# A gather ring of 16 slots: SyncE marks its slots in groups of four instead of one by one

## The reference

```python
def _rgcn_conv(x, W, Wroot, b, src, dst, etype):
    xs = x[src]                          # one row of 256 for each edge
    seg = dst * R + etype                # R = 8 relations
    sums = jax.ops.segment_sum(xs, seg, num_segments=N * R)
    cnt = jax.ops.segment_sum(jnp.ones_like(xs[:, 0]), seg, num_segments=N * R)
    mean = (sums / jnp.maximum(cnt, 1.0)[:, None]).reshape(N, R, -1)
    return x @ Wroot + b + jnp.einsum('nrd,rde->ne', mean, W)
# x + conv(relu(conv(layernorm(x)))), then a top-2 mixture of experts on top of it
```

## Time and profile before

| | us |
|---|---|
| Median of 3 runs | 2933.71 (2932.59 to 2935.83) |
| Profiled execution, span from the first to the last instruction | 3487.9 |
| PE busy (matmul) | 2472.0 (71%) |
| DVE busy | 1780.8 (51%) |
| ACT busy | 1225.2 (35%) |
| POOL busy | 1862.5 (53%) |
| Gathers of the two layers, busy on POOL | 1526.9 (1584 of them) |

### The profile page before, as it was taken

The page is one execution under the profiler, slowest core; times in us unless marked ns, Lnnn a source line. Parts: engine busy times, 40 slices in busy tenths (PEclk is TensorE's granted clock), DMA queues, the critical chain, the costliest instruction groups (busy, mean ns, idle before and its releaser), DMA issues.

```text
span 3487.9 us, 82172 instructions
## 1 busy us (share of the span) xinstructions
PE 2472.0 (71%) x19212; PEld 1832.7 (53%) x19213; DVE 1780.8 (51%) x4984; ACT 1225.2 (35%) x2344; POOL 1862.5 (53%) x1980
## 2 busy tenths in 40 slices
PE   1346787678687786346776587687877428999999
PEld 0113565356365564114564365465656327888887
DVE  7324455345355454124454354354545338787777
ACT  5202343134243342012343143152432126555554
POOL 1666566655655554666556656655563543333333
PEclk9557999589799898557998798798997559999999
DMA  6223323233332232223333333333335234322222
GB/s 216 80 83 112 88 87 91 85 87 89 87 88 87 86 89 64 86 84 97 98 104 97 94 100 99 94 105 95 101 100 163 102 115 132 96 73 71 71 70 59
DMA packets 165489, 333.24 MB, mean 96 GB/s; under 512 B 36078, under 2 KB 102346, under 8 KB 165288
## 3 DMA queue, kind: packets, MB, share of 16 engines
q0 software_dynamic: 91632, 247.48, 24.1%
q1 hardware_dynamic: 39912, 41.03, 4.0%
q10 hardware_dynamic: 33872, 43.92, 3.9%
HBM read 285.39 MB, written 49.07 MB: 96 GB/s over the span
## 4 chain that ended last, share of the span: by engine, by line
PE 44%; issue 22%; DVE 10%; another core or an unknown queue 9%; DVEq 7%; SPq 2%; ACT 2%; DMA 1%; ACTq 0%; POOLq 0%; POOL 0%
PE more_banks L1408 13%; PE sum_banks L1384 9%; PE sum_banks L1385 7%; PE more_banks L1535 4%; PE sum_banks L1535 3%; PE more_banks L1400 3%; PE sum_banks L1545 3%; DVEq L1044 3%; DVEq L1041 2%; DVE sels L1044 2%; DVEq L1027 1%; DVE stage L1079 1%; DVE sels L1036 1%; PE sum_banks L1426 1%
## 5 line engine op out<-in xcount | busy, mean ns | idle before, releaser
L509 POOL DMA_INDIRECT ring<-table,tabs x1584 | 1526.9, 964 | 1046.4 <-SPq L399 670.0
L1384 PE MATMUL sum_banks<-ring,sels 128*128 x2348 | 726.6, 311 | 630.1 <-issue 420.1
L1408 PE MATMUL more_banks<-weights,stage 128*128 128x256 f16 x5292 | 919.1, 290 | 22.0 <-issue 21.4
L1385 PE MATMUL sum_banks<-ring,sels 128*128 x2348 | 732.2, 313 | 41.5 <-issue 38.7
L1384 PEld LDWEIGHTS sum_banks<-ring,sels 128*128 128x128 f16 (+1 forms) x2348 | 242.4, 103 | 928.2 <-issue 896.9
L683 ACT ACTIVATE stage<-sum_banks,inv 128x256 f16<-128x256 f32 x784 | 328.1, 473 | 789.5 <-issue 384.9
L1408 PEld LDWEIGHTS more_banks<-weights,stage 128*128 128x128 f16 x5292 | 531.1, 104 | 135.3 <-issue 37.1
L1036 DVE SCALAR_TENSOR_TENSOR sels<-lane,win_off,tabs 128x256 f16<-128x256 f16 x792 | 349.4, 482 | 422.1 <-remote 181.9
L654 ACT ACTIVATE stage<-more_banks 128x1024 f16<-128x1024 f16 x392 | 402.0, 1026 | 419.1 <-remote 405.6
L1044 DVE TENSOR_SCALAR sels<-lane,win_off,tabs 128x128 f16 x780 | 260.6, 334 | 495.8 <-issue 339.6
L1079 DVE SCALAR_TENSOR_TENSOR stage<-sum_banks,inv,stage 128x256 f16<-128x256 f32 x784 | 347.0, 479 | 57.2 <-issue 40.2
(11 more groups left out here) (319 smaller groups left out, 2407.5 us busy)
## 6 DMA issues: line engine op xcount, KB each, us to landing
ring<-table,tabs POOLq DMA_INDIRECT x1584
weights<-L_ffn_W ACTq DMA_DIRECT2D x96, 178.5 KB
stage<-L_ffn_W ACTq DMA_DIRECT2D x16, 1024.0 KB, 5.0
edge_work<-lot_in SPq DMA_DIRECT2D x54, 260.0 KB
table<-edge_work ACTq DMA_DIRECT2D x49, 128.0 KB
lot_in<-sels SPq DMA_DIRECT2D x8, 260.0 KB
weights<-L_gnn_W SPq DMA_DIRECT2D x2, 1024.0 KB, 8.3
weights<-L_gnn_W ACTq DMA_DIRECT2D x2, 1024.0 KB
```

The lines of the kernel that those rows point to most:

```text
L509: pool.indirect_dma_start(ring_rows[:, b % RING, 0:2 * D], None, tables[layer], bass.IndirectOffsetOnAxis(row_tab[:, b:b + 1], 0)).then_in ...
L1384: pe.matmul(to[:, 0:D + 1], hot, ring_row[:, ds(at + D, D + 1)], start=first, stop=last, skip_group_check=True)
L1385: return pe.matmul(to[:, 0:D], hot, ring_row[:, ds(at, D)], start=False, stop=last, skip_group_check=True)
L1408: return [pe.matmul(ps_out[par], rows[:, xp * KD + k, :], w16[:, wp, k, r * D:(r + 1) * D], start=part == PART_ORDER[0] and n == 0, stop=p ...
```

## The change

SP marks four slots at once. The 16 slots are four groups of four (`GROUP`, `RING_GROUPS`). The four gathers of a group count on one semaphore, and `landed(g)` waits until it has the 64 counts of all four and adds four to `rows_ready`. `freed(g)` waits for the last step that reads the last block of the group (the table keeps every fourth entry only) and adds four to `slots_free`. The order is `freed(g)`, `landed(g + 2)`: two groups, eight blocks, as before. POOL waits before every fourth gather only, and then until all four slots are free. The number of turns of SP's loop stays 48, with four registers to load in place of 16. PE and DVE have the same instructions and the same waits as before. Later users of the gathers' semaphores (`scattered`) have other start values.

```diff
-    AHEAD = RING // 2
+    GROUP = 4
+    RING_GROUPS = RING // GROUP
+    AHEAD = RING_GROUPS // 2
...
-        gathered = [sem(f"gathered{s}") for s in range(RING)]
+        gathered = [sem(f"gathered{g}") for g in range(RING_GROUPS)]
...
-                def landed(turn, s):
-                    sp.wait_ge(gathered[s], turn * 16 + 16 * (USES[s] * layer + 1))
-                    sp.sem_inc(rows_ready[layer], 1)
+                def landed(turn, g):
+                    sp.wait_ge(gathered[g], turn * (16 * GROUP) + 16 * GROUP * (USES[g] * layer + 1))
+                    sp.sem_inc(rows_ready[layer], GROUP)
 
-                def freed(s):
-                    sp.wait_ge(steps_done[layer], sp.snap(regs[s], donate=True) & MASK)
-                    sp.sem_inc(slots_free[layer], 1)
-                for s in range(AHEAD):
-                    landed(0, s)
+                def freed(g):
+                    sp.wait_ge(steps_done[layer], sp.snap(regs[g], donate=True) & MASK)
+                    sp.sem_inc(slots_free[layer], GROUP)
+                for g in range(AHEAD):
+                    landed(0, g)
...
                 with sp.Fori(0, TURNS) as u:
-                    sp.load(regs, free_meta[0:1, ds(u * RING, RING)])
-                    for s in range(RING):
-                        freed(s)
-                        landed(u if s < AHEAD else u + 1, (s + AHEAD) % RING)
+                    sp.load(regs, free_meta[0:1, ds(u * RING_GROUPS, RING_GROUPS)])
+                    for g in range(RING_GROUPS):
+                        freed(g)
+                        landed(u if g < AHEAD else u + 1, (g + AHEAD) % RING_GROUPS)
...
                 for b in range(GATHERS):
-                    if b >= RING:
-                        pool.wait_ge(slots_free[layer], b - RING + 1)
+                    if b >= RING and b % GROUP == 0:
+                        pool.wait_ge(slots_free[layer], b - RING + GROUP)
                     pool.indirect_dma_start(ring_rows[:, b % RING, 0:2 * D], None, tables[layer],
-                                            bass.IndirectOffsetOnAxis(row_tab[:, b:b + 1], 0)).then_inc(gathered[b % RING], 16)
+                                            bass.IndirectOffsetOnAxis(row_tab[:, b:b + 1], 0)).then_inc(gathered[b % RING // GROUP], 16)
...
-            act.activation(free_meta, free_row[:, 0:GATHERS], ACT.Copy).then_inc(tabs_set, 1)
+            act.activation(free_meta, free_row[:, GROUP - 1:GATHERS:GROUP], ACT.Copy).then_inc(tabs_set, 1)
```

More of the change, by code:

```diff
@@ L45, in build_program @@
     GATHERS = BLOCKS + COUNT - 1
-    TURNS = (GATHERS - RING) // RING
-    OVER = GATHERS - RING - TURNS * RING
-    USES = [len(range(s, GATHERS, RING)) for s in range(RING)]
+    assert GATHERS % GROUP == 0
+    GROUPS_ALL = GATHERS // GROUP
+    TURNS = (GROUPS_ALL - RING_GROUPS) // RING_GROUPS
+    OVER = GROUPS_ALL - RING_GROUPS - TURNS * RING_GROUPS
+    USES = [len(range(g, GROUPS_ALL, RING_GROUPS)) for g in range(RING_GROUPS)]
     LOOKS = WINDOWS + 2 * COUNT
@@ L121, in build_program @@
         key_tab = tabs[:, GATHERS:3 * GATHERS + 4]
-        free_meta = tabs[0:1, 2 * GATHERS + 4:3 * GATHERS + 4].bitcast(i32)
+        free_meta = tabs[0:1, 2 * GATHERS + 4:2 * GATHERS + 4 + GROUPS_ALL].bitcast(i32)
         win_off = sb("win_off", [P, WINDOWS + 4])
@@ L306, in build_program @@
         routed, zs_ready = sem("routed"), sem("zs_ready")
-        assert len(set(USES[0:GROUPS])) == 1
-        spots_after = 16 * USES[0] * 2
+        assert GROUPS <= RING_GROUPS
+        spots_after = [16 * GROUP * n * 2 for n in USES]
         scattered = gathered[0:GROUPS]
@@ L390, in _ @@
             for layer in range(2):
-                regs = [sp.alloc_register(f"sp_free{layer}_{s}") for s in range(RING)]
-                def landed(turn, s):
-                    sp.wait_ge(gathered[s], turn * 16 + 16 * (USES[s] * layer + 1))
-                    sp.sem_inc(rows_ready[layer], 1)
-                def freed(s):
-                    sp.wait_ge(steps_done[layer], sp.snap(regs[s], donate=True) & MASK)
-                    sp.sem_inc(slots_free[layer], 1)
-                for s in range(AHEAD):
-                    landed(0, s)
+                regs = [sp.alloc_register(f"sp_free{layer}_{g}") for g in range(RING_GROUPS)]
+                def landed(turn, g):
[6 more added lines that the diff above has]
+                    landed(0, g)
                 if layer == 0:
@@ L404, in _ @@
                 with sp.Fori(0, TURNS) as u:
-                    sp.load(regs, free_meta[0:1, ds(u * RING, RING)])
-                    for s in range(RING):
-                        freed(s)
-                        landed(u if s < AHEAD else u + 1, (s + AHEAD) % RING)
[L409 to L414, removed]
+                    sp.load(regs, free_meta[0:1, ds(u * RING_GROUPS, RING_GROUPS)])
+                    for g in range(RING_GROUPS):
+                        freed(g)
+                        landed(u if g < AHEAD else u + 1, (g + AHEAD) % RING_GROUPS)
+                sp.load(regs, free_meta[0:1, TURNS * RING_GROUPS:(TURNS + 1) * RING_GROUPS])
+                for n in range(TURNS * RING_GROUPS, GROUPS_ALL - AHEAD):
+                    if n < TURNS * RING_GROUPS + OVER:
+                        freed(n % RING_GROUPS)
+                    landed((n + AHEAD) // RING_GROUPS, (n + AHEAD) % RING_GROUPS)
+                sp.sem_inc(rows_ready[layer], GROUP)
                 for r in regs:
@@ L437, in _ @@
             for g in range(GROUPS):
-                sp.wait_ge(scattered[g], spots_after + 32 * CHUNK * len(range(g, CHUNKS, GROUPS)))
+                sp.wait_ge(scattered[g], spots_after[g] + 32 * CHUNK * len(range(g, CHUNKS, GROUPS)))
             def load_lot(row):
@@ L1151, in z_rows @@
                 if c >= GROUPS:
-                    v.wait_ge(scattered[g], spots_after + 32 * CHUNK * (c // GROUPS))
+                    v.wait_ge(scattered[g], spots_after[g] + 32 * CHUNK * (c // GROUPS))
                 for i in range(CHUNK):
```

## The result

The changed kernel takes 2959.7 us (median of 4 runs, 2956.8 to 2962.1), the kernel before on the same chip 2933.7 us: ratio 1.0087, 95% interval 1.0073 to 1.0101. That is +26 us, where +13 us was forecast.

What follows compares the result with a forecast made beforehand. It took the timed runs as near POOL's floor of 1.25 us a gather, 989 us a layer. The middle of 18 us (lag account) and 7.6 us (ends) gave +13 us, 2947 us; 8-in-10 range 2922 to 2982 us.

Steps and rivals of the forecast that it cites:

- the check: Whole kernel: both layers at 989 us plus the first profile's other stretches give 2944 us, 10 us over the timed median.
- Parts 1, 2 and 5: SP's fewer marks, POOL's fewer waits, and the shared semaphore, register loads and table: no gain or cost.
- Part 3: `landed` waits for four gathers: a group's first block is marked up to 3.8 us later, so PE falls further behind.
- The term of the ends: At each layer's end the late landing lies on the path: 3.8 us, twice 7.6 us.
- account of the lag: PE's lag behind POOL over nine runs of tiles, limited by landing and ring: 9 us a layer, 18 us in all.
- costs nothing: Rival: PE never far enough ahead to miss three blocks, ring never full; 2934 to 2939 us, chance 0.22.
- every handover counts: Rival: each change between dense and thin runs costs 3.8 us; 34 us a layer, 68 us, 3002 us; chance 0.08.
- Taking the middle between 18 and 7.6 us: Total: between the lag account's 18 us and the ends alone, 7.6 us, if the ring is never full: +13 us.
- first case: Small loss at the layers' ends and partly in the ring: 2940 to 2958 us, chance 0.45.
- the shorter landing of 2.3 us: The skill's estimate for 128 KB against the trace's 2.9 us; said to move the sum by less than 1 us.
- DVE holding the transposes: Rival: DVE stands in `more_blocks` and PE's transposes wait, 36 us a layer; up to 2990 us, chance 0.05.
- Faster by relieving SP: Rival: POOL's slot waits are partly SP's lateness, half given back by one mark for four; 2916 us, chance 0.20.

Runs made afterwards that it cites:

- second profile: The kernel before, unchanged, profiled again; it spans 2933.1 us, where its first profile spans 3487.9 us.
- experiment 6: The changed kernel with `landed` marked three groups past the freed one in place of two; +27.0 us over the kernel before.
- the two halves: The kernel before with only `landed` marked by fours, +8.4 us, and with only `freed` marked by fours, +10.8 us.
- experiment 1: The kernel before with only `landed` marked by fours, each slot's own semaphore kept, `freed` slot by slot; +8.4 us, ratio 1.0034.

## Why the prediction came out as it did

**What bounds the kernel: right.** The gathers follow each other at little more than 1.25 us: layer 1 of the changed kernel is 1008.9 us where 791 x 1.25 = 989. The floor itself was set somewhat low. It went by the usual gather of 0.95 us, where the earlier trace rows have 964 ns on the average; with that it is 1000 us a layer, and the check would have come out at 2966 us, 32 us over the median in place of 10, a sign that something else in it was too long. The chain that ended last, by line, kernel before (second profile) and changed kernel:

```profile
by line: POOL ring L509 29.3%; issue 15.7%; PE sum_banks L1545 7.9%; PE more_banks L1408 7.3%; DMA ring<-table,tabs 5.2%; PE sum_banks L1384 4.3%; PE sum_banks L1535 4.0%; PE more_banks L1535 3.9%; POOL lot_in L533 3.3%; PE sum_banks L1385 
```

```profile
by line: POOL ring L513 28.0%; issue 14.9%; PE more_banks L1412 10.7%; PE sum_banks L1549 8.1%; PE sum_banks L1388 5.4%; PE sum_banks L1539 3.9%; PE more_banks L1539 3.9%; PE sum_banks L1389 3.8%; POOL lot_in L537 3.2%; PE more_banks L1404 
```

POOL's gathers lead it in both. What grows is PE's dense product, from 7.3% to 10.7% of the span: the path runs longer over PE before it goes back to POOL, as one would expect of a shallower ring.

**Parts 1, 2 and 5, at nothing: right as far as the runs can tell.** Groups of two cost +3.8 us with half of SP's marks, and gathers without a wait have the same 0.30 us in front as those with one.

**Part 3, landing late by 3.8 us at each handover: right in kind.** It was read directly as 15.5 to 19.2 us of lag.

**The term of the ends, 2 x 3.8 us: wrong.** Where PE waits for rows at the last gather, the layer would end later. It doesn't: with landing by four the gap from the last gather to the next layer is 23.2 us, as before,

```profile
1122.24 0.94 POOL L511 DMA_INDIRECT ring<-table,tabs  x1 [0.30 <-issue]
1145.42 1.14 POOL L511 DMA_INDIRECT ring<-table,tabs  x1 [22.23 <-DMA table<-edge_work]
```

and with freeing by four it is shorter, 20.5 us, since PE is less far behind.

```profile
1125.88 0.94 POOL L510 DMA_INDIRECT ring<-table,tabs  x1 [0.30 <-issue]
1146.40 1.13 POOL L510 DMA_INDIRECT ring<-table,tabs  x1 [19.58 <-DMA table<-edge_work]
```

PE is behind POOL at the ends of the layers, the rows had landed, and the term is 0. The sign that the prediction named for itself, a longer stretch between the layers, did not come. Its account of the lag had this the right way round, with a lag at the end of 17 us in place of 21. The row that said so was in hand: POOL had waited 1.5 us for a slot before the last gather, which the rival "costs nothing" used and the sum did not.

**The account of the lag, 18 us for both layers: right in kind, short in size, and wrong in taking both layers alike.** PE's surplus over POOL in tiles 36 to 42 was put at 20 us in both. ACT's copies of the turned means at the first and last couple of these tiles in the second profile of before, layer 0 and then layer 1:

```profile
804.63 1.03 ACT L654 ACTIVATE stage<-more_banks 128x1024 f16<-128x1024 f16 x1
...
901.25 1.02 ACT L654 ACTIVATE stage<-more_banks 128x1024 f16<-128x1024 f16 x1
...
1842.77 1.03 ACT L654 ACTIVATE stage<-more_banks 128x1024 f16<-128x1024 f16 x1
...
1930.64 1.02 ACT L654 ACTIVATE stage<-more_banks 128x1024 f16<-128x1024 f16 x1
```

From the first to the last of 28 couples it is 96.6 us in layer 0, 3.58 us each, and 87.9 us in layer 1, 3.25 each. At that pace 28 couples take 100 and 91 us, and POOL needs 62 x 1.25 = 78 us. So PE's surplus is 23 us in layer 0 and 14 us in layer 1. The other thin runs, read in the same way, have 24, 25 and 25 us in layer 0 and 14, 13 and 15 us in layer 1. Between least and most lag the prediction had 21 us for the ring before and 13 us after. In layer 0 the surplus is over both, so that what the groups take of the ring is lost at each thin run; in layer 1 it is well below the first and only just over the second, and layer 1 loses 3.9 us in all.

Put into the prediction's account in place of its own 18 to 21 us, these surpluses give an estimate of 14 us more of standing in layer 0 and 9 us more in layer 1, 23 us together, where the waits for slots grew by 22 and 4 us. The sum comes out and its parts do not: the account also has 36 us of standing in layer 0 before, where 22 were measured, and it has the loss of layer 0 too small. The theory gives the kind of the loss and where it falls, not its size in each layer. Layer 0's 26 us come as 2 us in the first gathers, 6 to 7 us of waits at each of the first three thin runs, 1 us at the last, and the gathers' own 4.5 us; "every handover counts" had 4 us down and 4 us up at each of the four, 34 us with the end. How it looks in layer 0, near the end of a thin run's gathers, kernel before and changed kernel:

```profile
683.71 0.94 POOL L509 DMA_INDIRECT ring<-table,tabs  x1 [0.30 <-issue]
685.09 0.95 POOL L509 DMA_INDIRECT ring<-table,tabs  x1 [0.44 <-SPq L399]
687.81 0.94 POOL L509 DMA_INDIRECT ring<-table,tabs  x1 [1.77 <-SPq L399]
689.49 0.94 POOL L509 DMA_INDIRECT ring<-table,tabs  x1 [0.73 <-SPq L399]
690.74 1.04 POOL L509 DMA_INDIRECT ring<-table,tabs  x1 [0.30 <-issue]
```

```profile
681.20 0.94 POOL L513 DMA_INDIRECT ring<-table,tabs  x1 [1.24 <-SPq L403]
682.45 0.95 POOL L513 DMA_INDIRECT ring<-table,tabs  x1 [0.30 <-issue]
...
687.96 0.94 POOL L513 DMA_INDIRECT ring<-table,tabs  x1 [2.05 <-SPq L403]
689.21 0.94 POOL L513 DMA_INDIRECT ring<-table,tabs  x1 [0.30 <-issue]
...
694.24 0.94 POOL L513 DMA_INDIRECT ring<-table,tabs  x1 [1.07 <-SPq L403]
```

Before, POOL is held at single gathers, in these rows at most 1.5 us longer than the usual gap of 0.30; with groups it issues four and stands, in these rows up to 1.8 us longer than usual, again and again.

**Taking the middle between 18 and 7.6 us: the step that failed.** It rested on the check, in which the timed time had no room for POOL to stand. That check set the layers at the floor and took everything else from the profiled execution as it was. The second profile has 67 us less outside the layers and 57 us more than the floor inside. The 36 us of standing for which the check "has no room" were 22 us, and they were there. Without that step the forecast would have been 2952 us, 8 us short. The other term of the middle, 7.6 us for the ends, does not exist. That the time fell within the range owes something to the range: 2960 us lies just over the 2940 to 2958 us that the prediction gave for its first case. The rival "every handover counts" came near in layer 0, 26 us where it had 34, and not in layer 1.

**A slip on the way.** With the shorter landing of 2.3 us the account moves by 1.2 us a layer, not by less than 1 us. Nothing hangs on it.

**The other rivals.** DVE holding the transposes: out by experiment 6. Faster by relieving SP: out, no grouping of any kind was faster. The shared semaphore, which the Trainium skill ("DMA: Bandwidth & Descriptors", "Why a DMA increments its semaphore by 16 and not by 1") advises against, has no cost of its own that shows here: with a semaphore for each slot kept, the two halves together are already at +19 us, groups of two, which share one as well, cost 3.8 us with all that they do, and what the sharing forces, the wait for the full 64, is the late landing of experiment 1.

## What to carry to other kernels

Marking slots of a ring in groups of n takes up to n - 1 slots from the producer and adds up to n - 1 transfers to the consumer's lag. In this kernel, with groups of four, that cost 4 us in the layer in which the surplus of a stretch (13 to 15 us) is about what the ring still holds (13 us by the estimate), and 26 us in the layer in which it is over what the ring held before (23 to 25 against 21 us). So find the stretches in which the consumer falls behind and its pace for every phase apart, and compare the surplus with the ring before counting semaphores: here SP had slack and there was nothing to win.

A profile whose span is far from the timed runs is first to be taken again. If there is only the one, its parts outside the disputed stretch are no steadier than those inside.

## What was not expected

The same kernel had one profiled execution of 3487.9 us and one of 2933.1 us, with the same 82172 instructions. In the long one gathers came at a steady 1.60 us in dense and thin tiles alike, in the other at 1.25 us with standing only in places; what held them at that pace was not found. The two layers, whose PE instructions are alike, differ by 0.3 us a couple in thin tiles (3.58 and 3.25 us in tiles 36 to 42). Most of it is the inverse counts of layer 0 and the waits for them: without both the same run takes 3.32 us a couple there.
